# Attention with a gated feed-forward: two head groups to a period, and six places for the exponentials

## The reference: what is computed

```python
def _L0_attn_ref(query, key, value, Wqkv, Wproj, bproj):   # 16 heads of 16; keys and values come from xn too
    mixed = x @ Wqkv.T
    ...
    attn = jnp.einsum('gqd,gkd->gqk', q, k) * norm
    attn = jax.nn.softmax(attn, axis=-1)
    ctx = jnp.einsum('gqk,gkd->gqd', attn, v)
    ...
    out = ctx @ Wproj.T + bproj
...
    h = jax.nn.gelu(jnp.einsum('lne,he->lnh', x, proj1) + proj1_bias, approximate=False)
    out = jnp.einsum('lnh,eh->lne', h, proj2) + proj2_bias
...
xn = _layernorm(x, axis=-1)
s = _L0_attn_ref(xn, ...)
g = _silu(_L0_ffn_ref(xn, ...))
x = x + s * g
```

## Time and profile before

| | |
|---|---|
| median of 3 runs | 136.43 us |
| the profiled execution's own time | 136.42 us |
| its span in the trace | 134.5 us |
| PE busy | 123.0 us (91%) |
| DVE busy | 89.3 us (66%) |
| ACT busy | 75.7 us (56%) |
| POOL busy | 50.8 us (38%) |
| share of PE in the chain that ended last | 70% |

### The profile page before, as it was taken

How to read it: one execution, slowest core, us unless ns; L and a number is a source line. 1 busy time by engine, 2 the same in 40 slices (tenths; PEclk the granted TensorE clock), 3 DMA queues, 4 the chain that set the end, 5 groups by cost and what they waited for, 6 DMA issues and landing times.

```text
span 134.5 us, 2614 instructions
## 1 busy us (share of the span) xinstructions
PE 123.0 (91%) x980; PEld 93.4 (69%) x980; DVE 89.3 (66%) x178; ACT 75.7 (56%) x115; POOL 50.8 (38%) x53
## 2 busy tenths in 40 slices
PE   6769979999997999999999999698999999999970
PEld 5449868988897889887677787465665566666450
DVE  0558974610000799999996999667668756858983
ACT  3044457879992011109467605649869787987710
POOL 3259203999995000002755660069604000004400
PEclk9999999999999999999999999999999999999998
DMA  4699879999999999200000000800000110110103
GB/s 123 201 407 425 224 163 150 153 158 152 172 181 184 163 170 174 51 0 2 5 0 0 0 15 10 301 11 7 17 0 0 44 39 0 44 41 2 44 2 117
DMA packets 7553, 13.29 MB, mean 99 GB/s; under 512 B 1012, under 2 KB 2676, under 8 KB 7284
## 3 DMA queue, kind: packets, MB, share of 16 engines
q1 hardware_dynamic: 7108, 12.85, 43.0%
q10 hardware_dynamic: 432, 0.27, 0.7%
HBM read 5.51 MB, written 1.05 MB: 49 GB/s over the span
## 4 chain that ended last, share of the span: by engine, by line
PE 70%; DVE 10%; ACT 8%; DMA 5%; issue 5%; SPq 1%; ACTq 0%; DVEq 0%
PE bank L590 48%; PE bank L706 10%; PE bank L658 6%; PE bank L678 6%; DMA wqkv_raw<-wqkv 5%; DVE negm L506 4%; ACT PT L431 4%; DVE cd L523 1%; DVE yh L548 1%; ACT cTh L443 1%; ACT xTh L375 1%; DVE rc L526 1%; DVE fin L565 1%; SPq L259 1%; ACT wqh L365 0%
## 5 line engine op out<-in xcount | busy, mean ns | idle before, releaser
L506 DVE TENSOR_REDUCE negm<-bank 128x4 f32<-128x1024 f32 x32 | 37.0, 1216 | 18.7 <-PE bank L658 18.6
L431 ACT ACTIVATE PT<-bank 128x1024 f32<-128x1024 f32 x32 | 30.7, 1019 | 6.6 <-PE bank L678 6.6
L340 POOL TENSOR_TENSOR hTl<-hG,hTh 128x512 fp32r<-128x512 f32 x16 | 20.3, 1289 | 26.1 <-ACT hTh L417 26.0
L350 POOL TENSOR_TENSOR bg<-gate,bps 128x256 f32<-128x256 f32 x8 | 5.9, 741 | 34.7 <-DVE gate L471 25.8
L706 PE MATMUL bank<-PT,VA 128*17 128x256 f32 x256 | 16.9, 382 | 0.0
L437 ACT ACTIVATE th<-yh 128x256 f32<-128x256 f32 x8 | 3.3, 418 | 23.0 <-DVE yh L548 23.0
L590 PE MATMUL bank<-w2h,hTh 128*128 128x256 f32 x64 | 14.8, 313 | 1.2 <-ACT VA L398 0.8
L678 PE MATMUL bank<-qs,ks 50*128 50x256 f32 x128 | 13.1, 312 | 1.7 <-ACT PT L431 1.7
L590 PEld LDWEIGHTS bank<-w2h,hTh 128*128 128x128 f32 x64 | 9.7, 190 | 6.5 <-issue 4.6
L413 ACT ACTIVATE hG<-bank,b1s 128x512 f32<-128x512 f32 x16 | 11.0, 689 | 5.5 <-PE bank L590 5.5
L523 DVE STREAM_TRANSPOSE cd<-bank 128x256 f32<-128x256 f32 x16 | 7.2, 447 | 10.5 <-PE bank L706 10.5
(11 more groups left out here) (72 smaller groups left out, 205.5 us busy)
## 6 DMA issues: line engine op xcount, KB each, us to landing
qs<-stage SPq DMA_DIRECT2D x12, 256.0 KB, 11.8
ks<-stage SPq DMA_DIRECT2D x12, 256.0 KB, 17.9
w_raw<-w SPq DMA_DIRECT2D x2, 1024.0 KB, 9.5
xs<-x SPq DMA_DIRECT2D x4, 256.0 KB, 5.9
xb<-x SPq DMA_DIRECT2D x1, 1024.0 KB, 5.3
out<-fin SPq DMA_DIRECT2D x8, 128.0 KB, 1.7
wqkv_raw<-wqkv SPq DMA_DIRECT2D x3, 256.0 KB, 6.9
wps<-wp SPq DMA_DIRECT2D x8, 32.0 KB, 8.2
```

Source lines behind the costliest of these rows:

```text
L340: nc.gpsimd.tensor_tensor(hTl[:, n % FC, :], hG[:, n % FC, :], hTh[:, n % FC, :].bitcast(f32), ALU.subtract).then_inc(h_lo, 1)
L350: nc.gpsimd.tensor_tensor(bg[:, u % 2, :], gate[:, u, :], bps[:], ALU.mult).then_inc(bg_done, 1)
L431: nc.scalar.activation(PT[:, w % 4], scores_of(*s), ACT.Exp).then_inc(exp_done, 1)
L506: nc.vector.tensor_reduce(negm[:, j, :, :, s[1] % 2, b].rearrange("p q a -> p a q"), scores_of(*s), axis=AX.X, op=ALU.max, negate=True).th ...
```

## The change

It rewrites the list of steps from `ST 0` on, so that a period holds two groups: two `ST`, the fillers of the period together, two more `ST`, then two `PV` one behind the other. In the last two groups the `PV` stand singly again. For that it adds or moves the following:

- Two more places for exponentials, `PT_more`, in the memory of `w1h`, which the last `F1` has read by then; ACT waits for that (`f1_made`) before it first writes there.
- Seven of the eight copies `cTh` go from ACT to POOL, as a CAST of 128 x 256, between POOL's bias steps; the last one stays on ACT with a semaphore of its own.
- The banks of the last stage: `F2` from tile 4 on alternates between 7 and 6, `PJ` uses 7 but for tiles 3 and 5 (bank 6) and tile 6 (bank 4), late `MT` uses 6.

```diff
-    for g in range(GROUPS):
...
+    for d in range(GROUPS // 2 - 1):
+        g = 2 * d
         order += [("ST", 2 * g), ("ST", 2 * g + 1)]
+        if d >= 4:
+            order += [("PJ", d - 4, 0), ("PJ", d - 4, 1), ("FIN", d - 4)]
+        order += [ffn.pop(0) for _ in range((2, 2, 2, 1, 1, 1, 0)[d])]
+        if d >= 2:
+            order.append(("TURN", d % 2, d // 2 - 1))
+        if d == 6:
+            order.append(("GATE",))
+        order += [("ST", 2 * g + 2), ("ST", 2 * g + 3)]
+        if d >= 1:
             order.append(("PV", g - 1))
...
+        order.append(("PV", g))
+        if d <= 1:
+            order.append(("MT", d + 2))
     assert not ffn
+
+    order += [("ST", 28), ("ST", 29), ("PJ", 3, 0), ("PJ", 3, 1), ("TURN", 1, 2), ("FIN", 3), ("PV", 13),
+              ("ST", 30), ("ST", 31), ("PJ", 4, 0), ("PJ", 4, 1), ("FIN", 4), ("PV", 14), ("TURN", 0, 3), ("PJ", 5, 0),
+              ("PV", 15), ("PJ", 5, 1)]
...
+        w1h_at = used[0]
         w1h = at("w1h", [P, KC, F], f32r)
+        PT_more = at("PT_more", [P, 2, 2, 2, SQ], f32, w1h_at)
...
+                elif kind == "F2" and s[1] >= TT // 2:
+                    home[s] = (7 - s[1] % 2,)
+                elif kind == "PJ":
+                    home[s] = (6,) if s[1] in (3, 5) else (7,)
...
+            n_gate = 0
+            for s in order[order.index(("ST", 0)):]:
+                if s[0] == "TURN":
+                    kc, j = s[1:]
+                    if high_of(kc, j)[0] is ct_hi:
+                        pool.wait_ge(turned, KC * j + kc + 1)
+                        if j >= 2:
+                            pool.wait_ge(pj_made, 2 * (j - 1))
+                        nc.gpsimd.tensor_copy(cTh[:, j % 2, kc, :], ctxT[:, kc, :]).then_inc(ct_hi, 1)
+
+                last = 4 if s == ("ST", 0) else s[1] if s[0] == "F2" and s[2] == 3 else TT if s[0] == "GATE" else 0
+                while n_gate < last:
+                    add_bias(n_gate)
+                    n_gate += 1
...
-                    if w >= 4:
-                        act.wait_ge(pv_made, (w - 4) // 2 + 1)
-                    nc.scalar.activation(PT[:, w % 4], scores_of(*s), ACT.Exp).then_inc(exp_done, 1)
+                    if w in (4, 5):
+                        act.wait_ge(f1_made, 2 * FC)
+                    if w >= 6:
+                        act.wait_ge(pv_made, (w - 6) // 2 + 1)
+                    nc.scalar.activation(exp_of(w), scores_of(*s), ACT.Exp).then_inc(exp_done, 1)
```

More of the change, by code:

```diff
@@ L198, in layer_kernel @@
         pv_made, cd_out, rc_done, norm_done = (sem(n) for n in ("pv_made", "cd_out", "rc_done", "norm_done"))
-        turned, ct_hi, ct_lo, wp_hi, wp_lo = (sem(n) for n in ("turned", "ct_hi", "ct_lo", "wp_hi", "wp_lo"))
+        turned, ct_hi, ct_last, ct_lo, wp_hi, wp_lo = (sem(n) for n in ("turned", "ct_hi", "ct_last", "ct_lo", "wp_hi", "wp_lo"))
         f2_made, b2_half, yh_done, th_done, gate_done, bg_done, xb_done = (
@@ L230, in banks @@
                     turn += 1
-                elif kind == "F2" or s[:2] == ("PJ", TT - 1):
+                else:
                     home[s] = (6,)
-                else:
-                    home[s] = (7,)
                 free[s] = list(dict.fromkeys(taken[k] for k in home[s] if k in taken))
@@ L245, in bank_of, with exp_of, high_of @@
             return bank[:, home[s][0], :]
+        def exp_of(w):
+            return PT[:, w % 6] if w % 6 < 4 else PT_more[:, w % 6 - 4]
         def scores_of(*s):
             return bank[:, home[s][0]:home[s][0] + 2, :].rearrange("p a (q c) -> p a q c", q=2)
+        def high_of(kc, j):
+            return (ct_last, 1) if (kc, j) == (1, HP // 2 - 1) else (ct_hi, KC * j + kc + 1)
         block = ctx.enter_context(nc.Block())
@@ L345, in _, with add_bias @@
             pool.wait_ge(bias_in, 48)
-            for u in range(TT):
+            def add_bias(u):
                 pool.wait_ge(gate_done, u + 1)
@@ L439, in _ @@
                     kc, j = s[1:]
-                    act.wait_ge(turned, KC * j + kc + 1)
-                    if j >= 2:
+                    if high_of(kc, j)[0] is ct_last:
+                        act.wait_ge(turned, KC * j + kc + 1)
                         act.wait_ge(pj_made, 2 * (j - 1))
-                    nc.scalar.activation(cTh[:, j % 2, kc, :], ctxT[:, kc, :], ACT.Copy).then_inc(ct_hi, 1)
+                        nc.scalar.activation(cTh[:, j % 2, kc, :], ctxT[:, kc, :], ACT.Copy).then_inc(ct_last, 1)
         @block.vector
@@ L555, in _ @@
                     kc, j = s[1:]
-                    dve.wait_ge(ct_hi, KC * j + kc + 1)
+                    dve.wait_ge(*high_of(kc, j))
                     nc.vector.tensor_tensor(cTl[:, j % 2, kc, :], ctxT[:, kc, :],
@@ L706, in _ @@
                             last = nc.tensor.matmul(bank_of(*s)[32 * m:32 * m + VW, 0:SQ], VA[:, 2 * b + kt, 4 * j + m, :],
-                                                    PT[:, w % 4, m % 2, kt, :], start=(kt == 0), stop=(kt == 1))
+                                                    exp_of(w)[:, m % 2, kt, :], start=(kt == 0), stop=(kt == 1))
                     last.then_inc(pv_made, 1)
@@ L711, in _ @@
                     j, qt = divmod(u, 2)
-                    pe.wait_ge(ct_hi, KC * j + kc + 1)
+                    pe.wait_ge(*high_of(kc, j))
                     if u == 0:
```

18 lines of the change are left out of this document (removed).

## The result

The changed kernel takes 134.58 us in the median of 4 runs (134.32 to 135.24), beside 136.19 us (135.93 to 136.46) for the kernel before: a ratio of 0.989, with a 95% interval of 0.985 to 0.993. Forecast were 135.3 us and -0.8%, with a range from 134.3 to 136.5. Run again as the first of the experiments, it came to 0.992 (0.988 to 0.995). The gain is real and small, between 0.5% and 1.5%.

The account below looks back on a forecast made before the run. PE was taken to set the pace, by its blocks' costs and its waits. From 136.42 us, -1.4 for changes of block and +0.3 for waits (-1.34 and +0.26 unrounded) gave 135.3 us, -0.8%, range 134.3 to 136.5.

Parts of the forecast that it names:

- Term A: Last stage, PE: changes between kinds of block cost 6.3 us instead of 7.7; -1.4 us, -1.34 unrounded.
- `PV` to `PV`: Last stage, PE: one `PV` directly behind another was taken to cost nothing, between nothing and 0.10 us.
- `PV` to score: Last stage, PE: going from `PV` to a score block was taken to cost 0.22 us, bounds 0.10 and 0.30.
- Rival 2: Last stage, PE: a second `PV` still costs the way out; +0.6, so 135.9 us; chance 0.10.
- Term B: Last stage: PE's waits sum to 4.4 us, 4.06 before; +0.3 us, +0.26 unrounded.
- DVE is late by 0.3: End of the stage: DVE works without a gap until 127.7 us, making PE's last wait 1.3 instead of 0.96.
- the wait at `F2 7 0`: PE waits 1.07 us for DVE's `mm` as POOL's bias work holds `ctxn`; without POOL 0.2.
- Rival 3: DVE's tail: a cast of 0.74 us delays each `TURN`; +0.5, 135.8 us, with two holds 136.4; chance 0.16.
- rival 4: DVE's tail: casts of 1.29 us outlast DVE's work; +2.7, 138.0 us; decides from about 1.0 us; chance 0.07.
- The copies on POOL: Last stage: seven copies of 0.41 us leaving ACT are worth nothing by themselves, since ACT had slack.
- The opening: Start of the stage: twelve products fill PE's idle time; waits 0.13 us at `ST 1` and 0.43 at `ST 5`.
- the 0.43 at `ST 5`: Opening: `ST 5` needs exponential 3, so it starts at 89.60 and not 89.27, a wait of 0.43 us.

Follow-up runs that it names:

- x5: The kernel before, its list of steps and banks kept, with six places for exponentials and seven copies on POOL: 1.013 of the kernel before.
- x6: Against the changed kernel, the first `PV` stands ahead of the second two `ST`, so the `PV` stand apart and fillers together: 1.005 of the kernel before.
- x0: The changed kernel run once more, nothing changed: 0.992 of the kernel before, median 135.52 us.
- x4: Against the changed kernel, POOL makes each of its seven casts twice, first to an unread scratch tile: 0.988 of the kernel before.
- x2: Against the changed kernel, all eight copies `cTh` are made by ACT, POOL does the bias work alone: 0.985 of the kernel before.
- x1: Against the changed kernel, `MT 3` stands ahead of `PV 1` and `PV 2` instead of behind them: 0.984 of the kernel before.
- x8: Against the changed kernel, POOL makes the copy of a `TURN` ahead of the same period's bias pair: 0.987 of the kernel before.
- x7: Against x1, `PV 15` stands directly behind `PV 14` and `PJ 5 0` behind both: 0.985 of the kernel before.
- x3: Against the changed kernel, four places for exponentials instead of six: 1.026 of the kernel before.

## Why the prediction was right, and where it was not

- **Term A, fewer changes of block, -1.34.** Right: 1.34 and 1.37 are left, with the two prices that were not in the trace: `PV` to `PV` is free (0.88, four waves of 0.22) and `PV` to score costs 0.10 out and 0.10 in (taken: 0.22 in all). That it fits so closely is in part luck: six such changes are 0.12 us cheaper than taken, and five runs of twelve that take 1.62 and not 1.60 make up 0.1. Rival 2 falls. x5 and x6 show that it is the list and within it the pairing that carries the gain. The Trainium skill's rule (TensorEngine Tiling (Array Packing), Key Properties: a change of mode drains the engine, a change of tile does not) agrees with these rows, in which blocks of one kind side by side pay nothing between them; that what is paid between different kinds is such a drain, the rows do not show.
- **Term B, waits, forecast +0.3, measured -0.5 and -0.1.** (From the rounded terms it is 4.38 - 4.06 = +0.32; the +0.26 of the sum does not follow from them.) Two steps of it failed. The first was "DVE is late by 0.3" at the end. The chain from `TURN 1 1` on was nearly well sized (12.2 us; measured 114.57 to 126.80 with 0.18 idle, so 12.05 of work). But `PV 15` starts 10.06 us after that `cTl`, where I had 9.8; 0.1 of that is the cast, which takes 0.40 and not 0.5, and the rest was not traced. So PE and not DVE ends last, and the wait stays at 0.97. The second is no error of mechanism: the wait at `F2 7 0` was sized for one standing of POOL's bias work against DVE, and x0 shows nearly that standing (1.02 against 1.07), the first profile a better one (0.63).
- **Rival 3's pricing was wrong in kind.** "`TURN 1 1`, `0 2`, `1 2`, `0 3` lie on DVE's late chain" is true of DVE's order, but only `TURN 1 1` waits for its cast; at the others the copy has long been made. x4 adds 0.15 us, where rival 3 had 0.5 for a cast of that length. The threshold of rival 4, a cast of about 1.0 us, was not tested.
- **The copies on POOL** were held to be worth nothing by themselves. By x2 they are worth 0.15 us of the stage, too little for the ratios to tell; x5 shows that they cost where the list is the old one.
- **The opening** kept its sign: twelve products where PE stood idle. From `ST 1` to `PV 0` PE waits for nothing, where the earlier trace rows had 1.5 us; what is left is the 0.43 at `ST 5`, as forecast.
- **The size of the whole.** -0.8% were forecast, -1.1% measured at first and -0.85% in x0, where the wait at `F2 7 0` was nearly as forecast. That the last figure comes so close is partly luck: in the stage, x0 gains 1.43 us where the terms had 1.34 - 0.32 = 1.0, and most of the difference is the last wait, 0.96 and not 1.3.

## What to carry to other kernels

When PE is busy all the time, compare the starts of its blocks with waves times the wave's price: what is left over is the price of changing the kind of block, and placing two blocks of a kind side by side earns it back, if there are buffers that let the engines around them run further ahead. Before such a reordering, look for short steps that fall behind the longer blocks on another engine, as `mm` did here: moving one matmul ahead of the pair (x1) shortened the stage by another 0.6 to 1.0 us. And an engine that waits 2 us and then works without a gap is not thereby the bound; doubling the suspected cost (x4) and taking the wait away (x8) tell it apart.

## What the runs showed of the hardware that was not expected

The time ahead of the stage varied by more than the change brought: in profiles of kernels that differ only behind it `ST 1` starts between 84.09 (x2) and 86.17 us (x4). The work there is the same, but TensorE's clock is not. The granted clock from 10 to 15 us was 1.00 in the kernel before, 0.68 in the changed kernel (first fence), and in x0:

```profile
5.00:10.00 5.00, 2.40 (x10) 0.99 (x9) 2.51 (x9) 1.51 (x4) 2.15 (x3) 0.89 0.99 363
10.00:15.00 5.00, 4.83 (x17) 4.38 (x18) 4.56 (x17) 1.96 (x6) 4.42 (x5) 0.50 0.99 389
```

There the clock stood at the lower of its two levels, 1.2 instead of 2.4 GHz, for the whole stretch from 10 to 15 us. What PE did before it: it was busy for 2.40 of the 5 us, waiting for the first inputs, against 2.85 in the kernel before and 2.25 in the changed kernel. From 20 us on all three have 1.00.

But that column alone does not order the kernels: the changed kernel, with 0.68, reaches `ST 1` at 84.86, ahead of x7 and x8, which have 1.00 and reach it at 85.22 and 85.27. PE's own rows do better. In the kernel before, where the column says 1.00:

```profile
12.81 1.05 PE L590 MATMUL bank<-xTh,wqh 128*128 128x512 f32 x2
13.66 0.71 PE L590 MATMUL bank<-xTh,wql 128*128 128x512 f32 x2
14.21 0.63 PE L590 MATMUL bank<-xTl,wqh 128*128 128x512 f32 x2
```

The first pair of these products takes 0.85 us from start to start, later pairs 0.46. Seven profiles with the new list start their first product at 9.8 to 10.2 us. In them the first quick pair of 128x512 starts at 12.31 us in x2, 13.50 in the changed kernel, 14.04 in x7, 14.36 in x8, 15.10 in x1, 16.04 in x0 and 16.19 in x4, and `ST 1` at 84.09, 84.86, 85.22, 85.27, 85.51, 86.05 and 86.17, in the same order. (The kernel before, at 14.21 and 85.10, is 0.1 us off that order; x3 and x6 start their first product later, at 10.74 and 12.11.) So most of what varies goes with how long PE's first products run at the slow price, and the granted clock of a stretch gives that only roughly. What makes that, and the arrival of the first inputs, differ from execution to execution was not examined.

The other thing is how sharp the lock between DVE and POOL is. `ctxn` takes 0.29 us alone. In the kernel before it starts 0.01 us into an `xb` (89.45 and 89.44), in x0 0.15 us into one (95.21 and 95.06), in the changed kernel 0.54 us (94.04 and 93.50), and each time it ends 0.15 us after that `xb`: 90.32 and 90.17, 95.93 and 95.78, 94.38 and 94.23. A `ctxn` that ran at a part of its speed beside POOL would not end at the same distance each time; these rows look like one that is held until POOL's instruction is over. So when the two meet 0.39 us later (0.54 and not 0.15 into the `xb`), PE waits 0.39 us less (0.63 and not 1.02).
